# A graph layer with residual and norm in fp32: K turned by way of DRAM, centring on ScalarE, four banks for projections

## What is computed

```
z_l = h @ W_lang.T;  z_g = h @ W_grav.T;  v = h @ W_V.T
zn  = z_l / max(norm(z_l), EPS)
A_l = max(zn @ zn.T, 0) * not_eye
A_g = exp(-max(sq + sq.T - 2 * z_g @ z_g.T, 0) / (2 * sigma**2)) * not_eye
K_l = A_l * adj / max(rowsum(A_l * adj), EPS)       # K_g the same from A_g
K   = sigmoid(gate) * K_l + (1 - sigmoid(gate)) * K_g
x   = layernorm(h + (K @ v) @ W_O.T)
```

## Time and profile before

| | us |
|---|---|
| median of three runs | 719.1 (718.97 to 719.81) |
| the profiled execution, its own time | 719.9 |
| its span in the trace | 717.8 |
| busy: TensorE / its weight loads | 695.8 / 574.8 |
| busy: VectorE / ScalarE / GpSimd | 515.4 / 346.4 / 110.8 |
| mean granted TensorE clock | 0.991 of full speed |
| moved by DMA | 90.75 MB |

### The profile page before, as it was taken

The page is one execution under the profiler, slowest core; times in us unless marked ns, Lnnn a source line. Parts: engine busy times, 40 slices in busy tenths (PEclk is TensorE's granted clock), DMA queues, the critical chain, the costliest instruction groups (busy, mean ns, idle before and its releaser), DMA issues.

```text
span 717.8 us, 10995 instructions
## 1 busy us (share of the span) xinstructions
PE 695.8 (97%) x3146; PEld 574.8 (80%) x3146; DVE 515.4 (72%) x1414; ACT 346.4 (48%) x643; POOL 110.8 (15%) x282
## 2 busy tenths in 40 slices
PE   8899999999999999999999999999999999999973
PEld 7688888888888888888888888888888888888852
DVE  4553877778777777777777777877777777876762
ACT  4333434536454544645545554644555463545445
POOL 3201001020111111020110111011110102011112
PEclk9999999999999999999999999999999999999998
DMA  9220634535453444544553444445344454353332
GB/s 286 51 60 30 154 104 118 154 112 147 148 153 115 143 136 124 153 123 125 144 141 124 128 136 152 123 128 153 125 145 126 124 153 124 96 154 96 65 86 99
DMA packets 105013, 90.75 MB, mean 126 GB/s; under 512 B 11040, under 2 KB 79136, under 8 KB 104992
## 3 DMA queue, kind: packets, MB, share of 16 engines
q1 hardware_dynamic: 104432, 88.93, 42.8%
q0 software_dynamic: 288, 1.05, 0.5%
q10 hardware_dynamic: 272, 0.52, 0.2%
HBM read 57.93 MB, written 32.54 MB: 126 GB/s over the span
## 4 chain that ended last, share of the span: by engine, by line
PE 94%; DVE 2%; ACT 1%; DMA 1%; issue 1%; POOL 0%; ACTq 0%; POOLq 0%; DVEq 0%
PE bank L951 90%; PE bank L1066 2%; PE bank L973 2%; DMA xs<-in_L_gnn_W_lang 1%; DMA out_y<-y 0%; ACT y L591 0%; DVE p_lo L679 0%; ACT m_hi L510 0%; DVE y L858 0%; ACT junk_a L583 0%; DVE m_lo L695 0%; DVE work L788 0%; DVE hT_raw L665 0%; ACT p_hi L500 0%; DVE hT_lo L673 0%
## 5 line engine op out<-in xcount | busy, mean ns | idle before, releaser
L951 PE MATMUL bank<-hT_lo,m_hi 128*128 128x512 f32 x512 | 168.0, 389 | 0.0
L543 ACT CAST p_hi<-bank 128x512 fp32r<-128x512 f32 x128 | 74.8, 584 | 127.9 <-PE bank L951 127.9
L738 DVE TENSOR_TENSOR p_lo<-bank,p_hi 128x512 fp32r<-128x512 f32 x128 | 87.7, 686 | 57.7 <-ACT p_hi L543 56.3
L951 PE MATMUL bank<-hT_hi,m_lo 128*128 128x512 f32 x320 | 124.5, 389 | 0.0
L951 PEld LDWEIGHTS bank<-hT_lo,m_hi 128*128 128x128 f32 x512 | 96.1, 188 | 20.0
L951 PE MATMUL bank<-p_hi,hT_hi 128*128 128x512 f32 x256 | 101.2, 395 | 0.0
L951 PE MATMUL bank<-wvo_hi,hT_hi 128*128 128x512 f32 x256 | 100.5, 393 | 0.0
L951 PE MATMUL bank<-wvo_lo,hT_hi 128*128 128x512 f32 x256 | 100.3, 392 | 0.0
L951 PE MATMUL bank<-wvo_hi,hT_lo 128*128 128x512 f32 x256 | 100.2, 392 | 0.0
L951 PE MATMUL bank<-p_lo,hT_hi 128*128 128x512 f32 x256 | 100.0, 390 | 0.0
L543 ACT CAST v_hi<-bank 128x512 fp32r<-128x512 f32 x64 | 37.6, 588 | 115.4 <-PE bank L951 115.4
(11 more groups left out here) (105 smaller groups left out, 1208.9 us busy)
## 6 DMA issues: line engine op xcount, KB each, us to landing
x_blk<-in_x SPq DMA_DIRECT2D x128, 128.0 KB, 3.0
x_nat<-in_x SPq DMA_DIRECT2D x32, 512.0 KB, 4.6
out_y<-y SPq DMA_DIRECT2D x32, 512.0 KB, 3.1
x_spill<-xs SPq DMA_DIRECT2D x30, 512.0 KB, 4.1
xq<-x_spill SPq DMA_DIRECT2D x120, 128.0 KB, 3.2
r_row<-r_spill SPq DMA_DIRECT2D x32, 128.0 KB, 4.2
work<-in_L_gnn_W_grav SPq DMA_DIRECT2D x2, 512.0 KB, 6.6
y<-in_L_gnn_W_O SPq DMA_DIRECT2D x2, 512.0 KB, 8.4
```

The lines of the kernel that those rows point to most:

```text
L543: nc.scalar.copy(dst, src).then_inc(proj_hi, 1)
L738: nc.vector.tensor_tensor(dst, src, hi.bitcast(F32), ALU.subtract).then_inc(proj_ready, 1)
L951: last = pe.matmul(dst, lhsT, rhs, start=(n == 0), stop=(n == len(steps) - 1))
```

## The change

K is turned another way. When both halves of K of a batch are done, `spill_k` stores the 256 KB to DRAM and `return_k` loads them back in four transfers, with 32-row blocks regrouped, in runs of 256 bytes; `turn_k` on VectorE transposes the 32x32 blocks. `kt_hi_part` and `kt_lo_part` then read SBUF, not a bank. Only the last pair keeps `k_turn`. To fit, everything of 256 x 256 (work, the mask, kt) is laid out with the two row tiles interleaved in blocks of 32; `gram` becomes one instruction for both row tiles, `turn_x` becomes two. The banks are dealt anew: four for projections, two for K V, two for X, and the tail's `gram_turn` and `k_turn` use the X banks. The centring goes from VectorE to ScalarE (`centre`). The inverse norms are stored as (t p) instead of (p t), in elements of 4 bytes. The mask comes in one transfer, into `r_row`, and is copied into its layout by GpSimd. The orders in the queues of all engines are rewritten: both K V tiles of a batch stand together, behind the X tiles; the first gram sum of the next pair, the turn of its X and ScalarE's `gauss` move to the end of the pair; mean and layer norm of batch 0 move to the next pair.

The diff, cut:

```diff
-        proj_bank = bank[0:3]
-        kv_bank = bank[3]
+        proj_bank = bank[0:4]
         x_bank = bank[4:6]
-        kt_bank = bank[6:8]
+        kv_bank = bank[6:8]
...
+            def spill_k(q, b):
+                if not live(q):
+                    return
+                sp.wait_ge(k_ready, upto(q, 4, 2 * b + 2))
+                sp.dma_start(k_spill[b].rearrange("h p f -> p h f"),
+                             wk(b, KER).rearrange("p (h f) -> p h f", h=NT)).then_inc(k_spilled[b], 16)
+
+            def return_k(q, b):
+                if not live(q):
+                    return
+                sp.wait_ge(k_spilled[b], 16 * (q + 1))
+                run = NT * BLK
+                for j in range(P // BLK):
+                    cols = k_spill[b].rearrange("h (i c) f -> c (h i) f", c=BLK)[:, :, run * j:run * (j + 1)]
+                    sp.dma_start(wk(b, COS)[j * BLK:(j + 1) * BLK].rearrange("c (k f) -> c k f", f=run),
+                                 cols).then_inc(kq_loaded[b], 16)
+
             def store_r(p, b):
                 sp.wait_ge(pool_steps, upto(p, 6, 3 * b + 1))
-                sp.dma_start(r_spill[b], rnorm[:, b]).then_inc(r_stored[b], 16)
+                sp.dma_start(r_spill[b].rearrange("t p -> p t").unsqueeze(2), rnorm[:, b].unsqueeze(2),
+                             allow_slow_non_contiguous=True).then_inc(r_stored[b], 16)
...
                 return_x(q, 1)
+                spread_r(q, 1)
+                load_blocks(p + 1, 1)
+                load_x(q, 0)
+                load_x(q, 1)
+                spill_k(q, 0)
                 load_blocks(p + 2, 0)
+                return_k(q, 0)
+                spill_k(q, 1)
                 store(q - 1, 0)
-                load_blocks(p + 1, 1)
-                spread_r(q, 1)
-                load_x(q, 0)
                 store(q - 1, 1)
-                load_x(q, 1)
+                store_r(p, 0)
                 spill_x(p, 0)
-                store_r(p, 0)
+                return_k(q, 1)
+                spread_r(p, 0)
                 return_x(p, 0)
-                spread_r(p, 0)
                 spill_x(p, 1)
                 store_r(p, 1)
...
-                layer_norm(q - 1, 1)
-                inverse_norms(p, 0)
-                floors(p, 0)
-                mean(q, 0)
-                inverse_norms(p, 1)
-                floors(p, 1)
-                mean(q, 1)
-                layer_norm(q, 0)
+                for b in range(2):
+                    mean(q - 1, b)
+                for b in range(2):
+                    layer_norm(q - 1, b)
+                for b in range(2):
+                    inverse_norms(p, b)
+                    floors(p, b)
...
+            def centre(p, b):
+                act.wait_ge(diag_ready, upto(p, 2, b + 1))
+                for t in range(NT):
+                    rows = x_plain(b)[:, t, G] if is_last(p) else x_of(b)[:, :, :, G, t].rearrange("p u j a -> p (u j) a")
+                    nc.scalar.activation(rows, rows, ACT.Identity, bias=x_diag[:, b, G, t:t + 1]).then_inc(centred, 1)
...
                 proj_hi_part(p, 1)
+                squares(q - 1, 0)
                 proj_hi_part(p, 2)
-                normalise(q - 1, 0)
                 proj_hi_part(p, 3)
-                gauss(q, 0)
+                proj_hi_part(p, 4)
+                gauss_scaled(q, 0)
                 squares(q - 1, 1)
-                proj_hi_part(p, 4)
                 proj_hi_part(p, 5)
-                gauss_scaled(q, 0)
                 proj_hi_part(p, 6)
                 proj_hi_part(p, 7)
                 gauss(q, 1)
-                normalise(q - 1, 1)
-                kt_hi_part(q, 0)
-                turn_hi(p + 1, 1 - parity, 0)
+                normalise(q - 1, 0)
+                gauss_scaled(q, 1)
                 save_x(p, 0, 0)
                 save_x(p, 0, 1)
-                gauss_scaled(q, 1)
+                normalise(q - 1, 1)
+                centre(p, 0)
+                kt_hi_part(q, 0)
                 save_x(p, 1, 0)
                 save_x(p, 1, 1)
-                kt_hi_part(q, 1)
+                if is_last(p):
+                    return
+                turn_hi(p + 1, 1 - parity, 1)
                 proj_hi_part(p, 8)
                 proj_hi_part(p, 9)
-                if is_last(p):
-                    return
-                squares(q, 0)
-                turn_hi(p + 1, 1 - parity, 1)
+                centre(p, 1)
+                kt_hi_part(q, 1)
                 proj_hi_part(p, 10)
                 proj_hi_part(p, 11)
-
+                turn_hi(p + 2, parity, 0)
+                gauss(p, 0)
+
+            turn_hi(1, 1, 0)
...
-                both = work[:, b, COS:GAUSS + 1].rearrange("p g (h k c) -> p k (g h) c", h=NT, c=BLK)
-                nc.vector.transpose(both, xq[:, b].rearrange("p (k m a) -> p k m a", m=2 * NT, a=BLK)).then_inc(xT_ready, 1)
+                    dve.wait_ge(kt_ready, upto(q - 1, 2, b + 1))
+                both = work[:, b, COS:GAUSS + 1].rearrange("p g (h i u c) -> p u i (g h) c", h=NT, u=NT, c=BLK)
+                for u in range(NT):
+                    ins = nc.vector.transpose(both[:, u], xq[:, b, u * WIDE:(u + 1) * WIDE].rearrange(
+                        "p (i m a) -> p i m a", m=2 * NT, a=BLK))
+                ins.then_inc(xT_ready, 1)
...
+            def turn_k(q, b):
+                if not live(q):
+                    return
+                dve.wait_ge(kq_loaded[b], BLKS * (q + 1))
+                dve.wait_ge(k_ready, upto(q, 4, 2 * b + 2))
+                nc.vector.transpose(wk(b, GAUSS).rearrange("p (t k c) -> p k t c", t=NT, c=BLK),
+                                    wk(b, COS).rearrange("p (k t a) -> p k t a", t=NT, a=BLK)).then_inc(kt_turned, 1)
...
                 proj_lo_part(p, 0)
-                turn_x(q, 0)
+                gram(q, 0, L)
                 proj_lo_part(p, 1)
-                gram(q, 0, G)
+                cosine_masked(q, 0)
+                gauss_masked(q, 0)
+                row_factors(q, 0)
                 proj_lo_part(p, 2)
-                inverse_masked(q, 0)
                 proj_lo_part(p, 3)
-                gauss_masked(q, 0)
-                gram(q, 0, L)
-                cosine_masked(q, 0)
+                turn_x(q, 1)
+                kernel_sum(q, 0)
+                inverse_masked(q, 1)
+                gram(q, 1, G)
                 proj_lo_part(p, 4)
-                row_factors(q, 0)
                 proj_lo_part(p, 5)
-                turn_x(q, 1)
+                gram(q, 1, L)
                 proj_lo_part(p, 6)
-                gram(q, 1, G)
-                kernel_sum(q, 0)
+                cosine_masked(q, 1)
                 proj_lo_part(p, 7)
                 gauss_masked(q, 1)
-                inverse_masked(q, 1)
-                gram(q, 1, L)
+                row_factors(q, 1)
+                turn_lo(p + 1, 1 - parity, 0)
+                kernel_sum(q, 1)
+                diagonal(p, 0)
+                turn_k(q, 0)
+                turn(p + 1, 1)
                 kt_lo_part(q, 0)
-                cosine_masked(q, 1)
-                row_factors(q, 1)
-                diagonal(p, 0)
-                kernel_sum(q, 1)
+                diagonal(p, 1)
+                if is_last(p):
+                    return
+                turn_lo(p + 1, 1 - parity, 1)
+                turn(p + 2, 0)
                 residual(q, 0, 0)
-                turn_lo(p + 1, 1 - parity, 0)
-                diagonal(p, 1)
-                kt_lo_part(q, 1)
                 residual(q, 0, 1)
                 proj_lo_part(p, 8)
-                if is_last(p):
-                    return
-                turn(p + 1, 1)
+                turn_k(q, 1)
+                proj_lo_part(p, 9)
+                kt_lo_part(q, 1)
+                inverse_masked(p, 0)
                 residual(q, 1, 0)
-                proj_lo_part(p, 9)
-                turn_lo(p + 1, 1 - parity, 1)
+                turn_x(p, 0)
+                gram(p, 0, G)
+                proj_lo_part(p, 10)
+                proj_lo_part(p, 11)
                 residual(q, 1, 1)
-                proj_lo_part(p, 10)
-                turn(p + 2, 0)
-                proj_lo_part(p, 11)
-
-            dve.wait_ge(adj_ready, NT)
+
...
                 for k in range(2 * DT):
                     project(p, parity, k)
                 value(p, parity, 0, 0)
-                k_turn(q, 0)
-                x_tile(p, parity, 0, 0)
-                x_tile(p, parity, 0, 1)
-                k_times_v(q, 0, 0)
-                x_tile(p, parity, 1, 0)
-                x_tile(p, parity, 1, 1)
-                k_turn(q, 1)
-                k_times_v(q, 0, 1)
+                for b in range(2):
+                    for t in range(NT):
+                        x_tile(p, parity, b, t)
                 if is_last(p):
                     return
                 value(p, parity, 0, 1)
-                k_times_v(q, 1, 0)
+                for t in range(NT):
```

(8 more changed lines are left out.)

250 lines of the change are left out of this document (139 added, 111 removed).

## The result

| | before | after |
|---|---|---|
| median | 719.2 us (718.97 to 719.81, four runs) | 805.0 us (801.74 to 810.31, four runs) |
| ratio to before, 95% interval | | 1.120 (1.114 to 1.126) |
| span of the profiled execution | 717.8 us | 802.9 us |
| mean granted TensorE clock | 0.991 | 0.942 |

A forecast was written before the change was run, and what follows sets the result against it. TensorE was taken to bound the kernel, busy 97% of the span. Loop -12.9, start -1.8 and end +2.2 gave -12.5 us: a span of 705.3, set against the median as 706.6 us, range 703.0 to 711.5.

The forecast's parts named there:

- the one on the norm store: Loop, DMA: the norm store in 256 4-byte pieces lands in 6.5 us, leaving X's return 2.1 us to spare.
- the rival's threshold of 9.2: Loop, DMA: above a norm store landing of 9.2 us, TensorE waits in every pair.
- the 2.1 of slack that I gave K of batch 1: Loop: K of batch 1 back near 31, turned at 33.8, split by 35.1, wanted at 37.2, 2.1 us to spare.
- Slower: the store of the norms: Loop rival: norm store lands in 11 us, X's return late, TensorE waits 1.8 us a pair, 734 us; chance 0.06.
- The loop, -12.9: Pairs 1 to 14: two turns of K leave TensorE, saving 0.92 us a pair, 12.9 us in all.
- Four banks and the hand-made queue of VectorE: Loop: with four projection banks and VectorE's new order, no wait is added; VectorE busy some 31 of 39.9 us.
- the place with 0.6 us to spare: End of a pair on VectorE: low part of value tile 10 done at 42.0, projection 2 needs its bank at 42.6.
- VectorE did not become the bound: Loop rival of no change: dearer VectorE work makes 0.8 us of wait a pair, 719 us; chance 0.04.
- Two terms that were added up wrongly: Loop: centring leaving VectorE counted as 1.1 us; K's round trip as 2 x 256 KB a pair on some 5.5 MB.
- The start, -1.8: Preparation: fewer bank waits bring the first W_V W_O product to near 28.3 from 30.13, -1.8 us (-0.5 to -3.3).
- The end, +2.2: Last pair: later last residuals, waiting for the store of y, add 1.0 us; TensorE's lower clock adds 1.2.

The follow-up runs named there:

- e4: e1 with the 8-byte norm store made twice, into two places, both waited for (256 pieces of 8 bytes): 711.3 us, ratio 0.989.
- e5_extra_packed: e1 plus an unread extra store of the norms ahead of its own, 256 packed 4-byte pieces, waited for only a pair later: 792.0 us, ratio 1.102.
- e6: The changed kernel with its 4-byte norm store issued from ScalarE's queue instead of SyncE's: two runs, 832.7 and 854.0 us, no ratio.
- e2: The changed kernel with K's return for batch 1 issued ahead of the stores of the norms and of X: 789.9 us, ratio 1.098.
- e1: The changed kernel with the norm store back to 128 pieces of 8 bytes, read by two strided instructions: 709.9 us, ratio 0.987.
- e5_extra_spread: e1 plus an unread extra store of the norms ahead of its own, 256 4-byte pieces placed 512 bytes apart: 710.7 us, ratio 0.989.
- f1: e1 with ScalarE's last-pair order changed: second kernel matrix's scaling before the previous pair's normalise, its squares before the last K split: 706.5 us, ratio 0.980.
- e3: The kernel before with only the norm store changed, to 256 pieces of 4 bytes: 726.0 us, ratio 1.0066.
- e8: e1 plus an unread extra store of the norms in two transfers, each 128 packed 4-byte pieces in rising order: 796.3 us, ratio 1.105.

## Why the prediction was wrong

**The step that failed is the one on the norm store**, in the part on DMA: "I take 6.5 (between these, a little for the extra pieces)". It failed twice.

- *The size.* 9.3 us, not 6.5, between the rival's threshold of 9.2 and its 11. I worked from the spread of 128 pieces and asked how many pieces there are. Number costs next to nothing (e4). What the step should have asked is where the pieces lie, and no row of before shows separately written neighbours of four bytes; the bound upward was therefore open, and I closed it with the number of pieces.
- *Who is held.* I let the store hold only SyncE, which waits for it, and X's return behind that wait. The X store I left at 4.1 us and K's return "near 31". Both were issued on time and landed late: the X store in 10.8, K's return at 440.40 - 401.4 = 39.0 us into the pair, 8 us behind the plan. Its turn ended at 39.7 instead of 33.8; of these 5.9 us the 2.1 of slack that I gave K of batch 1 took some, and TensorE waited the other 3.8. e5_extra_packed shows this with a store that nobody waits for within its pair, and e6 shows it across queues. This half carries the loss: by the rival's own sum a landing of 9.3 us holds TensorE for 0.1 us a pair.

**The rival "Slower: the store of the norms"** had the right instruction and the right sign with a chance of 0.06, but was mis-sized as well: 1.8 us a pair, 734 us, against 5.9 a pair and 805. It named X's return and TensorE's wait at projection 2; the wait came at K V, through K's return. Only when that return is moved (e2) does the rival's wait appear in every pair. And it left out the clock, which adds 2.0 us on average to waits of 3.7. Its counter-argument, that 128 pieces have landed in 3.1 us, says nothing on pieces of another layout. The Trainium skill's row on transfers under 512 B (DMA: Bandwidth & Descriptors, Specifications), which I set beside it, does not separate the cases either: pieces of 8 bytes, spread words of 4 bytes and K's runs of 256 bytes are all under 512 B, and e1, e5_extra_spread and K's return in e1 (3.2 us for 64 KB) are all cheap.

**The rest can be read from e1**, in which only that step is mended. Its span is 707.7, the prediction's 705.3.

- *The loop, -12.9.* Right. 578.77 / 2552 = 0.2268 us a product, 39.9 a pair, against 40.86: 14 x 0.95 = 13.3. The last pair starts at 634.9, where the prediction's terms give 649.3 - 12.9 - 1.8 = 634.6:

```profile
634.91 0.39 PE L1030 MATMUL bank<-hT_lo,m_hi 128*128 128x512 f32 x1
```

- *Four banks and the hand-made queue of VectorE.* Right: no wait at the place with 0.6 us to spare. A turn of K takes 708 ns (taken: 620 to 700) and a centring 506 ns (taken: 450), both a little over, both covered:

```profile
L907 DVE STREAM_TRANSPOSE work<-work 128x512 f32<-128x512 f32 x30 | 21.2, 708 | 0.7 <-DMA work<-k_spill 0.6
...
L589 ACT ACTIVATE xs<-xs,x_diag 128x256 f32<-128x256 f32 x64 | 29.1, 506 | 3.0 <-DVE x_diag L797 3.0
```

The same row says that K's round trip is hidden: VectorE waits for it 0.6 us in the whole kernel, against 77.6 in after. VectorE did not become the bound.

- *Two terms that were added up wrongly, without a cost.* The centring that leaves VectorE is 4 x 346 ns = 1.4 us, not 1.1. K's round trip is stored and loaded, so it adds four times 256 KB a pair, not two: the bytes moved go from 90.75 to 106.49 MB, 1.05 MB a pair. e1 carries them too.
- *The start, -1.8.* The first W_V W_O product starts at 28.25, predicted 28.3. But pair 0 begins 3.0 us earlier than before (34.52 for 37.50 in the chains), near the far end of my range, as the slow stretch behind the old waits shrank too. Of that, 1.81 is given back at the start of pair 1, at projection 2, by a wait that I had not seen: TensorE has only the rest of pair 0 and two projections to do while the first X goes through DRAM.

```profile
28.25 0.47 PE L1030 MATMUL bank<-hT_hi,v_hi 128*128 128x512 f32 x1 [0.96 <-DVE hT_lo L750]
...
78.98 0.50 PE L1030 MATMUL bank<-hT_lo,m_hi 128*128 128x512 f32 x1 [1.81 <-DVE v_lo L786]
```

- *The end, +2.2.* Right in kind, 2 us short. The tail takes 72.8 us from 634.9; predicted were 68.5 + 2.2 = 70.7. K V of the last pair starts at 684.93, 50.0 for 48.4, and behind the idle stretch the clock is at half, as said. The last residuals start at 63.2, not at 59.9: the wait for the store of y has grown to 6.78 us, which is what f1 cuts.

```profile
685.00:688.00 3.00, 3.00 (x7) 2.42 (x8) 0.10 (x1) 0.00 (x0) 0.00 (x0) 0.50 0.51 175
```

## What to carry to other kernels

When a layout is changed, ask of every store what lies next to each piece in DRAM, not only how many pieces and bytes there are: a transfer of 1 KB can hold up one of 512 KB. Where a term has no row of its own and others queue behind it, price it also by what happens if everything behind it is as late as it is, and give that more than a small chance. And a repeated wait of some 4 us on TensorE cost about half as much again here through the clock.

## What the runs showed of the hardware

- 256 words of 4 bytes, written as pieces of their own side by side in DRAM, land in 9.0 to 9.8 us at the median (after, e2, e3, e5_extra_packed, e6), and two rows of 128 in 9.0 and 8.4 (e8). The same words 8 or 512 bytes apart land in 4.9 to 5.9 us, 128 neighbouring pieces of 8 bytes in 5.4.
- While the packed words are written, other stores and loads land late too, from the same queue or from another: in the kernels with the new order the X store takes 9.5 to 11.5 us instead of 5.2 to 6.1. In one such stretch of after the DMA engines are recorded busy 0.76 of the time and move 11 GB/s.
- Which part of the chip holds them (the engines, the way to memory or the memory itself), and whether it is because two neighbours share an aligned word of 8 bytes, was not told apart; the runs had 4-byte pieces only at distances of 4, 8 and 512 bytes.
- In after, thirteen of TensorE's fourteen waits in the loop (3.1 to 4.8 us) were followed by 7 to 14 products that started mostly 0.43 us apart, then 0.227 again. The number does not go with the length of the wait: behind 3.14 us (at 395.72) it was fourteen, behind 3.15 us (at 579.89) seven. Behind the shortest, 2.26 us (at 122.82), it was none. Over the loop it comes to 2.0 us a pair.
